# An eight-image ViT tower on one core: attention laid out anew, with values in 88-token chunks and even and odd heads in turn

## The chip, the cores and the metric

The kernel runs on one core of one Trainium2 chip. The metric is the device time in microseconds of one execution, lower is better. Times are medians over the runs shown.

## What is computed

Eight small images become 66 tokens each (two class tokens and 64 patches) of width 192. Tokens then pass one attention block with complex scores and a four-layer encoder. This is the reference, cut to the encoder layers that the change touches (B is 8, s is 66, H is 12 heads of DK = 64, F = 768, L = 4):

```python
for i in range(L):
    nx = t5_layer_norm(h, ln1[i])
    q = (nx @ attn_q[i]).reshape(b, s, H, DK)
    k = (nx @ attn_k[i]).reshape(b, s, H, DK)
    v = (nx @ attn_v[i]).reshape(b, s, H, DK)
    scores = jnp.einsum('bqhd,bkhd->bhqk', q, k) + bias
    attn = jax.nn.softmax(scores, axis=-1)
    ctx = jnp.einsum('bhqk,bkhd->bqhd', attn, v).reshape(b, s, H * DK)
    h = h + ctx @ attn_o[i]
    nx = t5_layer_norm(h, ln2[i])
    y = jax.nn.relu(nx @ ffn_wi[i]) @ ffn_wo[i]
    if i in MOE_LAYERS:        # layers 1 and 3, 8 experts, top 2
        y = y + moe_ffn(nx.reshape(-1, d), gate_w[mi], moe_w1[mi], moe_w2[mi]).reshape(b, s, d)
        mi += 1
    h = h + y
```

## The kernel before

Activations stay in SBUF, transposed: features on partitions, tokens on the free axis. The batch is cut into two halves of four images, NT = 264 tokens each; the first argument of nearly every stage is the half (0 or 1), and one half's small work is placed between the other half's large matmuls. The generator `stages()` yields one hand-written list of stages, and each engine walks that same list in the same order and issues its own part of each stage. So on every engine the order is that of the list; waits are semaphores with counts that are worked out from the list.

The stages that matter here, each for a half `hf` and a layer:

- `qk`: the queries (i = 0) or keys (i = 1), 6 groups of 5 matmuls with 264 columns. ACT copies each group from a bank of the family `pa` (three banks) to `qk`.
- `scores` for one image `b`: 12 products, one per head, with 64 rows of contraction (even heads on partitions 0 to 63, odd heads on 64 to 127), into the two banks `ps`. DVE adds the bias into `prob` (twice, L1227) and takes the maxima (L1062); POOL subtracts them (L622). With the next image's scores, ACT does the exponentials (L914), DVE the sums and reciprocals (L1067, L1068), POOL the scaling (L628). `scores_end` does these last three for image 3.
- `v` for one image: the values, tokens as stationary operand and 384 weight columns as moving one, 2 groups of 5 matmuls; ACT copies each group from `pa` to `vtok` (L1006).
- `tp`: 12 transposes of the probabilities into two `pa` banks, copied by ACT to `probT` (L909). `pv`: 12 products of `probT` and `vtok`, left by DVE in two parts in `wide` (L1238, L1239).
- `o_tail`, `o_main`: the output projection, 12 and 18 matmuls, added to `hT` by DVE.
- `squares` (ACT), `norm` (PE, then DVE L1084, then POOL L634) and `scale` (PE, then DVE L1102, L1072 to L1074) are the normalisation; the last of them makes `xs`, which the next `qk` or `hid` waits for.
- `hid` and `y_tail`, `y_main`: the feed-forward block; ACT writes each hidden group twice (L1022, L1023) and DVE subtracts (L1250). Its banks are shared with `pa` and `ps`.
- `split`: ACT (L934) and POOL (L613) cut loaded weights into two parts. `warm(n)`: n matmuls of 512 columns on zeros, whose result nobody reads.

In layers 0 and 2 all four `scores` and `v` of half 0 come before `qk` of half 1, and half 1's four scores are then interleaved with `tp` and `pv` of half 0. In layers 1 and 3 (with experts) the four `scores` and `v` of a half come in turn, then the six groups of `hid` of the other half (or of the same half), then `tp` and `pv`.

## Time and profile before

| | us |
|---|---|
| median of 3 runs | 766.58 (756.33 to 770.01) |
| the profiled execution | 758.47 |
| its span, first to last instruction | 755.7 |
| PE busy in it | 704.8 |
| DVE busy | 445.1 |
| ACT busy | 406.6 |
| POOL busy | 352.2 |
| mean granted TensorE clock | 0.972 of full |

PE is TensorE's matmuls, PEld its weight loads, DVE is VectorE, ACT ScalarE, POOL GpSimd. A span and a start are microseconds from the first instruction. Ends of matmuls are modelled, so the distance between the starts of two groups is a better price than the time beside a group. Instructions that issue a DMA are not counted as busy, though the engine spends time on them.

### The profile page before, as it was taken

The numbers are of one execution on the slowest core, as the hardware profiler recorded it, in microseconds if no ns is written. First come the engines' busy times: TensorE is split into PE (matmuls) and PEld (weight loads), VectorE is DVE, ScalarE is ACT, GpSimd is POOL, SyncE is SP. The second block draws the span as 40 slices with busy tenths as digits, with TensorE's granted clock in tenths as the row PEclk, the third lists the DMA queues.
The fourth block names the chain that finished last, engine by engine and source line by source line (L and its number), as shares of the span: only waits on it lengthen the run. The fifth ranks groups of instructions, "written<-read, shape, count | busy, mean of one in ns | idle before, by whom it ended". The sixth has DMA issues, their size and how long they took to land.

```text
span 755.7 us, 16388 instructions
## 1 busy us (share of the span) xinstructions
PE 704.8 (93%) x6735; PEld 626.9 (83%) x6735; DVE 445.1 (59%) x941; ACT 406.6 (54%) x913; POOL 352.2 (47%) x327
## 2 busy tenths in 40 slices
PE   6976999899899999899999999998999999999995
PEld 4853578788787989899999888887889898999995
DVE  0348435386556486676556645764765865666664
ACT  1387335542456365677767355444554647767642
POOL 2357525472466244336675333515743533544520
PEclk9997899998999999999999999989999999999998
DMA  7321001020220204243345030002211134233200
GB/s 211 88 74 43 2 2 33 1 85 1 69 78 18 59 3 131 81 126 116 119 143 147 3 84 1 2 2 74 74 43 33 28 105 123 83 116 91 89 1 22
DMA packets 36609, 49.20 MB, mean 65 GB/s; under 512 B 6155, under 2 KB 27575, under 8 KB 36023
## 3 DMA queue, kind: packets, MB, share of 16 engines
q1 hardware_dynamic: 33259, 43.49, 20.1%
q10 hardware_dynamic: 3276, 4.67, 2.0%
q8 instruction: 53, 0.87, 0.5%
q14 instruction: 21, 0.17, 0.1%
HBM read 47.70 MB, written 0.45 MB: 64 GB/s over the span
## 4 chain that ended last, share of the span: by engine, by line
PE 72%; DVE 9%; ACT 8%; POOL 5%; issue 3%; DMA 2%; SPq 0%; POOLq 0%; ACTq 0%; DVEq 0%
PE pd L684 35%; PE pa L684 23%; PE ps L684 9%; PE pa L715 4%; POOL w L613 1%; DVE xn L1102 1%; POOL prob L622 1%; ACT wide L1022 1%; POOL wo L613 1%; ACT w L934 1%; ACT wqkv L934 1%; DVE xs L1072 1%; DVE xs L1074 1%; ACT pa L1023 1%; ACT csq L983 1%
## 5 line engine op out<-in xcount | busy, mean ns | idle before, releaser
L613 POOL TENSOR_TENSOR w<-raw,w 128x384 fp32r<-128x384 f32 x140 | 141.8, 1015 | 132.0 <-ACT w L934 124.1
L684 PE MATMUL pd<-wide,w 128*128 128x264 f32 x1200 | 156.0, 286 | 0.1
L684 PEld LDWEIGHTS pd<-wide,w 128*128 128x128 f32 x1200 | 149.2, 188 | 0.9 <-DVE wide L1250 0.9
L684 PE MATMUL pa<-xs,w 128*128 128x264 f32 x810 | 120.7, 289 | 10.3 <-DVE wide L1250 6.6
L684 PEld LDWEIGHTS pa<-xs,w 128*128 128x128 f32 x810 | 107.1, 190 | 14.9 <-DVE wide L1250 8.6
L1250 DVE TENSOR_TENSOR wide<-pa,wide 128x264 fp32r<-128x264 f32 x144 | 62.1, 432 | 40.4 <-ACT pa L1023 38.0
L622 POOL TENSOR_TENSOR prob<-prob,mx 66x792 f32<-66x792 f32 x36 | 55.4, 1543 | 45.9 <-DVE mx L1062 45.6
L1022 ACT ACTIVATE wide<-pa 128x264 fp32r<-128x264 f32 x144 | 56.8, 394 | 35.0 <-PE pa L684 34.8
L628 POOL TENSOR_TENSOR prob<-prob,rc 66x792 f32<-66x792 f32 x36 | 54.4, 1513 | 44.1 <-DVE rc L1068 44.1
L684 PE MATMUL ps<-xs,w 128*128 128x264 f32 x480 | 74.3, 285 | 0.5 <-DVE prob L1227 0.5
L613 POOL TENSOR_TENSOR wqkv<-raw,wqkv 128x384 fp32r<-128x384 f32 x48 | 49.6, 1034 | 48.0 <-ACT wqkv L934 45.2
L1138 DVE TENSOR_TENSOR pd<-pd,vtok 128x264 f32<-128x264 f32 x64 | 43.6, 681 | 39.5 <-PE pd L684 39.4
L684 PE MATMUL pa<-xs,wqkv 128*128 128x264 f32 x480 | 61.7, 287 | 4.7 <-DVE xs L1074 4.0
L684 PEld LDWEIGHTS ps<-xs,w 128*128 128x128 f32 x480 | 64.6, 188 | 1.3 <-issue 1.2
L684 PEld LDWEIGHTS pa<-xs,wqkv 128*128 128x128 f32 x480 | 59.3, 188 | 7.6 <-DVE xs L1074 6.6
L684 PE MATMUL pa<-wqkv,xs 128*66 128x384 f32 x320 | 63.5, 345 | 0.0
L684 PE MATMUL pd<-warm_x,warm_w 128*128 128x512 bf16 x191 | 59.2, 429 | 0.0
L902 ACT ACTIVATE qk<-pa 128x264 f32<-128x264 f32 x102 | 39.4, 390 | 36.8 <-PE pa L684 36.5
L634 POOL TENSOR_TENSOR rs<-var,exponent 88x3 f32<-88x3 f32 x22 | 18.7, 849 | 85.6 <-DVE var L1084 85.6
L1023 ACT ACTIVATE pa<-pa 128x264 f32<-128x264 f32 x144 | 56.6, 393 | 0.0
L934 ACT ACTIVATE w<-raw 128x1536 fp32r<-128x1536 f32 (+1 forms) x40 | 52.6, 1321 | 7.4 <-PE pd L684 3.9
L1006 ACT ACTIVATE vtok<-pa 66x384 f32<-66x384 f32 x64 | 29.8, 482 | 46.5 <-PE pa L684 46.4
(126 smaller groups left out, 1149.4 us busy)
## 6 DMA issues: line engine op xcount, KB each, us to landing
raw<-in_moe_w_dram SPq DMA_DIRECT2D x16, 576.0 KB, 4.2
raw<-in_moe_w_dram SPq DMA_DIRECT2D x16, 384.0 KB, 3.5
raw<-in_moe_w_dram SPq DMA_DIRECT2D x32, 192.0 KB, 3.9
vtok<-cw_rows ACTq DMA_DIRECT2D x4, 1056.0 KB, 6.0
raw<-in_attn_o_dram SPq DMA_DIRECT2D x4, 576.0 KB, 4.0
raw<-in_ffn_wo_dram SPq DMA_DIRECT2D x4, 576.0 KB, 4.1
vtok<-in_patches_dram SPq DMA_DIRECT2D x2, 768.0 KB, 7.9
raw<-in_attn_q_dram SPq DMA_DIRECT2D x4, 384.0 KB, 3.6
```

Source lines behind the costliest of these rows:

```text
L613: ins = nc.gpsimd.tensor_tensor(low, whole, high.bitcast(F32), ALU.subtract)
L622: nc.gpsimd.tensor_tensor(p, p, m.unsqueeze(2).to_broadcast([S, H, S]), ALU.subtract).then_inc(sub_ready, 1)
L628: nc.gpsimd.tensor_tensor(p, p, r.unsqueeze(2).to_broadcast([S, H, S]), ALU.mult).then_inc(prob_ready, 1)
L684: return nc.tensor.matmul(out_ap, lhsT, rhs, start=first, stop=last)
L715: last = nc.tensor.transpose(bank[0:S, j * S:(j + 1) * S], probs(u)[:, g * HG + j, :], ident[0:S, 0:S])
L902: nc.scalar.activation(dst, src, ACT.Copy).then_inc(a_free, 1)
L934: nc.scalar.activation(hi, src, ACT.Copy).then_inc(chunk_hi, 1)
L1006: nc.scalar.activation(vtok[0:S, hf * HALF_B + b, n * F // 2:(n + 1) * F // 2], bank_a()[0:S, 0:F // 2], ACT.Copy).then_inc(a_free, 1)
L1022: nc.scalar.activation(wide[hf][:, 0, m, :], bank, gate_fn)
L1023: nc.scalar.activation(bank, bank, gate_fn).then_inc(h_ready, 1)
L1138: done(nc.vector.tensor_tensor(part, part, weight, ALU.mult))
L1250: nc.vector.tensor_tensor(wide[hf][:, 1, m, :], places["h"][n][0][:, 0:NT], wide[hf][:, 0, m, :].bitcast(F32), ALU.subtract).then_inc(h_fr ...
```

## The change

There are four parts; all are within the encoder layers.

1. `scores` takes both `ps` banks first and issues even and odd heads in turn, where before all six even heads came ahead of all six odd ones.
2. `v` is computed for three chunks of 88 tokens in place of four images of 66. ACT copies a chunk to a staging tile, waits for its own copy, and issues two DMAs that move the rows to their images in `vtok`. `pv` waits for these DMAs (`v_moved`). Staging reuses other tiles; for that half 1 gets queries and keys of its own (`qk_late`), and DVE waits for half 0's moves before its first `pv`.
3. The list is rearranged. In layers 0 and 2 half 1's `qk` moves between the scores, or behind the first `tp` and `pv`, of half 0; `o_tail` comes between half 1's scores; and image 3 of half 1 is transposed only after the feed-forward block of half 0. In layers 1 and 3 the two parts of `hid` come between scores, and `tp` of image 0 comes ahead of scores of image 3.
4. Of 191 `warm` matmuls 143 are left: 17 fewer in layer 0, 21 in layer 2, 5 in each of layers 1 and 3.

```diff
+VC, VCN = 3, NT // 3
+V_MOVES = (((0, 0, 0, S), (1, 0, S, VCN - S)),
+           ((1, VCN - S, 0, 2 * S - VCN), (2, 0, 2 * S - VCN, 2 * VCN - 2 * S)),
+           ((2, 2 * VCN - 2 * S, 0, 3 * S - 2 * VCN), (3, 0, 3 * S - 2 * VCN, S)))
+V_PARTS = (1, 2, 2, 1)
...
                 elif name == "v":
-                    b = stage[3]
+                    c = stage[3]
                     pe.wait_ge(chunk_split, chunks_until("qkv", stage[2], 2))
                     for n in range(2):
                         cols = slice(n * F // 2, (n + 1) * F // 2)
-                        tok = slice(b * S, (b + 1) * S)
+                        tok = slice(c * VCN, (c + 1) * VCN)
                         pairs = split_pairs(wqkv[:, 0, 2], wqkv[:, 1, 2], xs[hf][:, :, tok], cols)
-                        product(bank_a()[0:S, 0:F // 2], [(x, w) for w, x in pairs], a_full)
+                        product(bank_a()[0:VCN, 0:F // 2], [(x, w) for w, x in pairs], a_full)
...
                     cols = slice(b * S, (b + 1) * S)
-                    for g in range(2):
-                        bank = bank_s()
-                        row = slice(DK * g, DK * g + DK)
-                        for j in range(HG):
-                            last = mm(bank[0:S, j * S:(j + 1) * S], qk[row, 0, j, cols], qk[row, 1, j, cols], True, True)
-                        last.then_inc(s_full, 1)
+                    pair = [bank_s(), bank_s()]
+                    for j in range(HG):
+                        for g in range(2):
+                            row = slice(DK * g, DK * g + DK)
+                            last = mm(pair[g][0:S, j * S:(j + 1) * S], qk_of[hf][row, 0, j, cols], qk_of[hf][row, 1, j, cols], True, True)
+                            if j == HG - 1:
+                                last.then_inc(s_full, 1)
...
                     layer, b = stage[2:4]
-                    if b == 0:
-                        pe.wait_ge(a_free, groups_after(A_GROUPS, ("v", hf, layer, HALF_B - 1)))
+                    pe.wait_ge(v_moved[hf][b], 16 * V_PARTS[b] * (layer + 1))
...
                     for n in range(2):
-                        nc.scalar.activation(vtok[0:S, hf * HALF_B + b, n * F // 2:(n + 1) * F // 2], bank_a()[0:S, 0:F // 2],
+                        nc.scalar.activation(rows_of[:, c, n * F // 2:(n + 1) * F // 2], bank_a()[0:VCN, 0:F // 2],
                                              ACT.Copy).then_inc(a_free, 1)
+                    act.wait_ge(a_free, groups_after(A_GROUPS, stage))
+                    for b, to, at, rows in V_MOVES[c]:
+                        act.dma_start(vtok[to:to + rows, hf * HALF_B + b, :], rows_of[at:at + rows, c, :]).then_inc(v_moved[hf][b], 16)
...
                 elif name == "pv":
+                    if hf == 0 and stage[3] == 0 and stage[2]:
+                        for b in range(HALF_B):
+                            dve.wait_ge(v_moved[0][b], 16 * V_PARTS[b] * (stage[2] + 1))
```

The first place is PE at the head of layer 2, from the last of half 0's `qk` on. `ps<-qk` are scores, `pa<-wqkv,xs` values, `pa<-xs,wqkv` queries and keys, `pa<-ident,prob` transposes, `pd<-ident,rs` the `scale` matmuls. Before:

```order
L684 MATMUL ps<-qk 66x66 x12
L684 MATMUL pa<-wqkv,xs 66x384 x10
L684 MATMUL ps<-qk 66x66 x12
L684 MATMUL pd<-ident,rs 128x88 x3
L684 MATMUL pa<-wqkv,xs 66x384 x10
L684 MATMUL ps<-qk 66x66 x12
L684 MATMUL pa<-wqkv,xs 66x384 x10
L684 MATMUL ps<-qk 66x66 x12
L684 MATMUL pa<-wqkv,xs 66x384 x10
L684 MATMUL pd<-warm_x,warm_w 128x512 x6
L684 MATMUL pa<-xs,wqkv 128x264 x60
```

After the change the same stretch (from the second `scores` on) reads:

```order
L743 MATMUL ps<-qk 66x66 x12
L743 MATMUL pd<-ident,rs 128x88 x3
L743 MATMUL pa<-wqkv,xs 88x384 x10
L743 MATMUL ps<-qk 66x66 x12
L743 MATMUL pa<-xs,wqkv 128x264 x30
L774 MATMUL pa<-ident,prob 66x66 x12
L743 MATMUL ps<-qk 66x66 x12
L743 MATMUL pd<-probT,vtok 64x66 x12
L743 MATMUL pa<-xs,wqkv 128x264 x30
```

Half 1's queries have moved ahead of half 0's fourth scores, right behind the third, and no `warm` stands ahead of them.

The second place is ACT at the end of half 1's scores in layer 2: `sq<-hT` is `squares`, `probT<-pa` the copy behind `tp`, `prob<-prob` an exponential. After the change:

```order
L1066 ACTIVATE qk<-pa 88x384 [waits a_full] x2
L1070 DMA vtok<-qk 22x768 [waits a_free]
L1070 DMA vtok<-qk 66x768
L973 ACTIVATE prob<-prob 66x792 [waits sub_ready]
L1004 ACTIVATE sq<-hT 128x528 [waits d_full,d_free]
L968 ACTIVATE probT<-pa 66x396 [waits a_full] x4
```

Here `squares` stands ahead of the copies behind half 1's first two `tp`; in the list before it stood behind them. The two DMA rows are new on ACT's queue.

The third place is ACT in the first half of layer 3, between half 0's values and the end of the first part of `hid`, after the change (`wide<-ps`, `wide<-pa` are `hid`):

```order
L1066 ACTIVATE v_rows_wide<-pa 88x384 [waits a_full] x2
L1070 DMA vtok<-v_rows_wide 44x768 [waits a_free]
L1070 DMA vtok<-v_rows_wide 44x768
L973 ACTIVATE prob<-prob 66x792 [waits sub_ready]
L1088 ACTIVATE wide<-ps 128x264 [waits h_full]
L1089 ACTIVATE ps<-ps 128x264
L1088 ACTIVATE wide<-pa 128x264 [waits h_full]
L1089 ACTIVATE pa<-pa 128x264
```

The exponential of image 0 now stands behind two chunks' copies and four DMA issues, and `hid` behind it; before, `hid` came only after all values.

## Rows read from the trace of the kernel before

**Rows 1.** The page: the span, and PE's busy time and share.

```profile
span 755.7 us, 16388 instructions
PE 704.8 (93%) x6735; PEld 626.9 (83%) x6735; DVE 445.1 (59%) x941; ACT 406.6 (54%) x913; POOL 352.2 (47%) x327
```

**Rows 2.** Windows: length, busy PE, PEld, DVE, ACT, POOL, clock, DMA share, GB/s.

```profile
110.30:205.00 94.70, 88.12 (x907) 75.38 (x905) 52.88 (x100) 42.92 (x86) 45.34 (x38) 0.95 0.11 33
205.00:291.10 86.10, 84.34 (x919) 74.39 (x920) 54.26 (x120) 47.45 (x99) 45.95 (x39) 1.00 0.19 54
171.40:187.80 16.40, 16.37 (x191) 13.46 (x191) 10.11 (x21) 4.33 (x9) 3.18 (x3) 0.80 0.01 1
```

**Rows 3.** Groups by shape: xcount, busy us, mean ns of one, idle before and its releaser.

```profile
L684 PEld LDWEIGHTS pa<-xs,wqkv 128*128 128x128 f32 x480 | 59.3, 188 | 7.6 <-DVE xs L1074 6.6 <-ACT qk L902 0.7
...
L684 PEld LDWEIGHTS pa<-wqkv,xs 128*66 128x66 f32 x320 | 41.8, 138 | 11.8
...
L1006 ACT ACTIVATE vtok<-pa 66x384 f32<-66x384 f32 x64 | 29.8, 482 | 46.5 <-PE pa L684 46.4
```

**Rows 4.** The chain that ended last, layer 1: start, us, PE group of values.

```profile
265.29 1.89 PE pa L684 x10
```

**Rows 5.** PE timeline in layer 0: transposes, scores, pv, values, by starts.

```profile
154.75 0.86 PE L715 MATMUL pa<-ident,prob 66*66 66x66 f32 x12
155.53 1.47 PE L684 MATMUL ps<-qk 64*66 64x66 f32 x24
156.93 0.92 PE L684 MATMUL pd<-probT,vtok 66*64 66x66 f32 x24
157.78 1.95 PE L684 MATMUL pa<-wqkv,xs 128*66 128x384 f32 x10
```

**Rows 6.** The tile cw_rows: DMA issues on ACT's queue (ns min/median/max), landing (us).

```profile
L1030 ACTq DMA_DIRECT2D cw_rows<-cw x4: 312/320/576, 282.5 to 628.0; - x4
...
DMA to landing us min/median/max: 5.5/6.0/6.7
```

**Rows 7.** Timeline of layer 2: what half 1's queries wait for.

```profile
442.58 1.47 PE L684 MATMUL ps<-qk 64*66 64x66 f32 x24 [0.48 <-ACT qk L902]
...
447.41 1.28 ACT L914 ACT_TABLE_LOAD   x1
...
450.95 0.81 DVE L1102 SCALAR_TENSOR_TENSOR xn<-hT,vec,pd 128x264 f32<-128x264 f32 x2
...
453.72 0.43 DVE L1074 TENSOR_TENSOR xs<-xn,xs 64x264 fp32r<-64x264 f32 x1
...
458.01 1.47 PE L684 MATMUL pd<-warm_x,warm_w 128*128 128x512 bf16 x6
...
459.12 7.64 PE L684 MATMUL pa<-xs,wqkv 128*128 128x264 f32 x60
```

**Rows 8.** Timeline of layer 2: half 1's scores, hid, o_tail of half 1.

```profile
467.84 1.47 PE L684 MATMUL ps<-qk 64*66 64x66 f32 x24
...
505.44 0.96 PE L684 MATMUL pa<-xs,w 128*128 128x264 f32 x5
...
513.21 1.62 PE L684 MATMUL pd<-wide,wo 128*128 128x264 f32 x12
```

**Rows 9.** PE timeline: layer 3's first queries.

```profile
522.55 1.61 PE L684 MATMUL pa<-xs,wqkv 128*128 128x264 f32 x11 [1.53 <-DVE xs L1074]
```

**Rows 10.** The same columns as rows 2, for the second half of layer 1.

```profile
260.90:285.50 24.60, 24.60 (x263) 21.65 (x263) 22.48 (x57) 13.82 (x30) 12.51 (x10) 1.00 0.03 6
```

**Rows 11.** DVE timeline, layer 1: y_main's add of half 1, then of half 0.

```profile
239.36 0.43 DVE L1142 TENSOR_TENSOR hT<-pd,hT 128x264 f32<-128x264 f32 x1
...
247.38 0.43 DVE L1074 TENSOR_TENSOR xs<-xn,xs 64x264 fp32r<-64x264 f32 x1
...
285.05 0.43 DVE L1142 TENSOR_TENSOR hT<-pd,hT 128x264 f32<-128x264 f32 x1
```

**Rows 12.** The same columns, instructions that touch the tile prob alone.

```profile
260.00:276.00 16.00, 0.00 (x0) 0.00 (x0) 10.59 (x15) 2.60 (x3) 9.48 (x7) 1.00 0.01 4
```

More of the change, by code:

```diff
@@ L174, in stages @@
                 yield ("squares", 1, "encoder")
-                beside = [[("norm", "encoder", 0)], [("scale", "encoder", 0), ("squares", "ln1")], [("norm", "ln1", 0)], [("scale", "ln1", 0)]]
-            else:
-                beside = [[("norm", "ln1", layer)], [("scale", "ln1", layer)], [], []]
-            for b in range(HALF_B):
-                yield ("scores", 0, layer, b)
-                for x in beside[b]:
-                    yield (x[0], 1) + x[1:]
-                yield ("v", 0, layer, b)
@@ new lines, in stages @@
+                yield ("v", 0, 0, 0)
+                yield ("norm", 1, "encoder", 0)
+                yield ("v", 0, 0, 1)
+                yield ("scores", 0, 0, 1)
+                yield ("scale", 1, "encoder", 0)
+                yield ("squares", 1, "ln1")
+                yield ("v", 0, 0, 2)
+                yield ("scores", 0, 0, 2)
+                yield ("norm", 1, "ln1", 0)
+                yield ("tp", 0, 0, 0)
+                yield from warm(2)
+                yield ("pv", 0, 0, 0)
@@ L195, in stages @@
+            yield ("squares", 0, "ln2")
             yield ("tp", 1, layer, 0)
-            yield ("o_tail", 0, layer)
+            yield from warm(2)
             yield ("pv", 1, layer, 0)
+            yield ("norm", 0, "ln2", layer)
             yield ("tp", 1, layer, 1)
             yield ("scores_end", 1, layer)
-            yield ("o_main", 0, layer)
-            yield ("squares", 0, "ln2")
-            yield from warm(1)
+            yield from warm(2)
             yield ("pv", 1, layer, 1)
@@ L204, in stages @@
             yield ("tp", 1, layer, 2)
[L205 removed]
+            yield ("scale", 0, "ln2", layer)
             yield ("pv", 1, layer, 2)
[L207 to L211 removed]
+            yield from warm(2)
             yield from hid(0, layer, 0)
@@ L215, in stages @@
             yield ("squares", 0, "ln1")
+            yield ("tp", 1, layer, 3)
+            yield from warm(2)
+            yield ("pv", 1, layer, 3)
             yield ("o_tail", 1, layer)
```

133 lines of the change are left out of this document (89 added, 44 removed).

## The prediction, made before the changed kernel was run

> **What bounds the kernel now.** I read the page's totals first. PE is busy for 704.8 us of a span of 755.7 us, 93%, and no other engine passes 59% [rows 1]. That says where to look, not what a saved matmul is worth, so I read windows over single stages next. Layer 0, from its first queries to those of layer 1, is 94.7 us long with PE busy for 88.1; layer 1's attention and first feed-forward part is 86.1 us long with PE busy for 84.3 [rows 2]. There is nearly no idle time on PE in either. But a shorter window tells more: in the second half of layer 1, from the first bias add to the end of the first feed-forward block, DVE is busy for 22.5 of 24.6 us [rows 10]. There PE and DVE finish together, and work that leaves PE alone buys little. (The windows' order of engines is PE, PEld, DVE, ACT, POOL.)
>
> Last I read the timeline around the waits. In layer 2 half 1's `xs` are ready at 453.72 + 0.43 = 454.15, yet PE takes its queries only at 459.12, since all of half 0's scores and values stand ahead [rows 7]. That is what the rearrangement uses. At layer 2's end it is the other way about: `hid` at 505.44, `o_tail` of half 1 at 513.21 and layer 3's queries at 522.55, the last behind a wait of 1.53 us for DVE's `xs` [rows 8, 9]. One more thing stands in the windows: the stretch 171.4 to 187.8 of layer 0, all transposes, `pv` and `warm`, ran at a granted clock of 0.80, so part of it at 1.2 GHz where the layer else has 2.4 [rows 2].
>
> **The terms on PE.** Scores of one image take 156.93 - 155.53 = 1.40 us before, and transposes 0.78 (155.53 - 154.75) [rows 5]. No row of before shows twelve heads alternating between the two halves of the rows. The nearest is `pv`: also twelve f32 products of 66 columns, whose outputs alternate between partitions 0 to 63 and 64 to 127; it takes 157.78 - 156.93 = 0.85 us [rows 5]. The ends are 1.40 (no overlap at all) and 0.70 (two heads always at once). I take 0.85, a gain of 0.55 on each of 8 x 4 = 32 images, 17.6 us.
>
> A rule of the Trainium skill bears on this: TensorEngine Tiling (Array Packing), Theoretical Speedup, gives up to 2x for a small dimension of at most 64. By that rule the term would be 32 x 0.70 = 22.4 us; by the `pv` row it is 17.6. I keep the row's.
>
> Values: ten matmuls, one stage, take 1.89 us [rows 4]. A layer had eight such stages and now has six; 8 fewer in all, 15.1 us. Against this the stationary part has 88 columns, not 66. Weight loads take 138 ns with 66 and 188 with 128 [rows 3], so 88 cost about 18 ns more; if nothing hid that, 240 matmuls would give back 4.3 us. Loads lie beside matmuls mostly, so I take nothing, and keep 10.8 to 15.1.
>
> `warm`: six take 459.12 - 458.01 = 1.11 us [rows 7], so 48 fewer are 8.9 us of PE. Where they only filled a wait this is worth nothing; I count it only inside the stages below.
>
> Together 17.6 + 15.1 + 8.9 = 41.6 us of PE. If PE alone set the time, 758.5 would become 716.9.
>
> **What is added.** ACT's copies fall from 64 to 48, each 0.48 us [rows 3], 7.7 us less. It gets 48 DMA issues. ACT's issues take 0.32 us in the median and 0.58 at most [rows 6]: 15.4 to 27.6 us, at a guess 0.4 each, so 0.8 us per chunk, plus a wait of some 0.1 for its own copy. ACT is a queue in order: behind these stand the exponential, then `hid`. The landing I bound by the 6.7 us of the slowest DMA of that queue [rows 6]; `pv` of an image comes 8 us and more after its chunk, so landing costs nothing. Without that cover it would be up to 6 us in each of 8 half-layers.
>
> **Layer 2, step by step.** Scores of image 0 start at 442.6 [rows 7]. PE then has three scores (2.6 us), three chunks of values (5.7), and the small matmuls of `norm` and `scale` (about 1.6): it is out of work at 452.5. On ACT, two chunks' copies and four DMA issues end at about 449.6; only then comes the table load of 1.28, which stood at 447.41 before [rows 7], and the exponential (0.9): 451.8. DVE's sum and reciprocal take 1.2; then the scaling takes 454.15 - 450.95 = 3.2 us as before [rows 7]: `xs` at 456.2. PE waits some 3.6 us there. Then come 7.3 us of queries and keys, two transposes (1.6), one scores (0.85), two `pv` (1.7) and a bare wait of 0.7 for the copy of the second transposes: half 1's scores start at 468.3, not at 467.84 [rows 8], with two `tp` and two `pv` already done.
>
> From there to `hid` it was 505.44 - 467.84 = 37.6 us [rows 8]. It loses 2.2 (scores), 3.8 (values), 1.9 (ten `warm`), 4.1 (a transpose of half 0, two of its `pv`, and image 3 of half 1, moved out), and about 2.5 of slow clock as in the alike stretch of layer 0: 23.1. New waits come in: `squares` stands ahead of the copies of half 1's first transposes on ACT and waits for DVE to add `o_main`, behind a bias add, a maximum and a sum (2.5 us); `xs` come late, behind the last sum and the two passes over a `pv` on DVE (3 us). So 28.7, and `hid` at 497.0. Then 7.8 us to the end of the block, as before [rows 8], and the moved image in the open: transposes, two `warm`, copy, `pv` and DVE's two passes, 3.7 us. `o_tail` at 508.5 for 513.21, and unchanged 9.3 us after it [rows 8, 9] layer 3 at 517.8: **4.7 us gained**.
>
> **Layer 0.** Same list, but half 1's `xs` need four dependent small stages. They now queue behind chunk copies on ACT and behind a scaling of probabilities on POOL, so I put them at 141.0, about 2 us later than before. With both `tp` and `pv` done ahead, scores of half 1 come at 148.4, and with layer 2's 49.5 us from there layer 1 starts at 197.9 in place of 205.0 [rows 2]: **7 us gained**.
>
> **Layers 1 and 3.** First half: DVE needs about 3 us of softmax per image (15 of 16 long instructions of four images are 10.59 us [rows 12], and a short one each besides). With that four times, the scaling, six `hid` subtractions, the tail's add and one `pv` it has from 214 on some 22 us in a row, so `y_main` of half 1 can be added at 236.2 at best where it was at 239.36 [rows 11]; with ACT's queue (third piece of the order) I put it at 237.8. But behind it `tp` of image 1 waits for `squares`, and POOL makes the root only behind a scaling, so `xs`, 247.81 before [rows 11], come at 247.3: 0.5 gained. Second half: DVE keeps its 22.5 busy of 24.6 us [rows 10], so at most about 2 up to 285.05 [rows 11] and something behind it, where the three `pv` no longer wait: 2.5. Two layers, **6 us gained**.
>
> **The clock.** The new waits of 2 to 4 us are of a kind that this trace has few of, and after thin stretches it shows a clock of 0.80 over 16.4 us, 3.3 us lost [rows 2]. I charge 2 us in each of layers 0 and 2: **4 us lost**.
>
> **The sum.** 758.5 - 4.7 - 7.0 - 6.0 + 4.0 = 744.8 us against the profiled execution's own 758.47. Its median neighbours are higher (756.33 to 770.01, median 766.58), so the ratio of 0.982 gives 752.8 us. About 28 of 41.6 us taken off PE turn into waits.
>
> **The rivals.**
> - *PE decides all the same.* For it speak 97% busy PE in layer 1 [rows 2] and that DVE's 22.5 us contain short gaps. Then most of 41.6 us comes through: 22 to 41 us, say 30, so 736. The clock loss would be gone as well.
> - *Evacuation decides.* The Trainium skill, TensorEngine Tiling, PSUM Bottleneck, says that tiling speeds up TensorE but not the evacuation of PSUM. By the windows, as a mechanism of this kernel: DVE's softmax per image is 3 us [rows 12] where PE's scores and values per image fall from 3.3 to 2.3, so DVE sets the pace of all 32 images; with the 15 us of ACT's issues on that path too, gain 0 to 6, 762. The trace agrees with the rule in layer 1's second half [rows 10].
> - *No overlap.* Scores stay at 1.40: only the values are left, and if half of their 15.1 us hides, the gain is 7.5: 759.
> - *Slower.* The place is the rearranged stretch of layers 0 and 2. PE waits for half 1's `xs` and again for `squares`; if the granted clock falls to 1.2 GHz in each such wait and stays there for the queries behind it, 7.3 us of them take 14.6. Twice per layer in two layers this is up to 29 us, and with it the gains above are gone from about 14 us on; at 29 it ends at 774. For it: 0.80 in a stretch with no long wait at all [rows 2]. Against it: large matmuls bring the clock back.
>
> **How the numbers follow.** A gain of 6 to 22 us, the forecast, has a chance of 0.46; PE decides 0.22; evacuation or no overlap 0.14; slower 0.18. A measurement of this kernel can tell about 2% from no change, 15.3 us here, which cuts my forecast case in two: 0.21 above it, 0.25 below. Faster by over 2%: 0.21 + 0.22 = 0.43. Slower by over 2%: 0.15 of the 0.18. The rest, 0.42, is within 2%. For the range I take PE decides at 33 us (733) and the slower case at its middle (771), which leaves out about 2 in 10. The forecast's own range is 744 to 761.
>
> **What would show it.** In the changed profile: scores groups of 12 at starts 0.8 to 0.9 us apart from what follows; values 1.9 us per ten, 240 matmuls; PE waiting 3 to 4 us for L1074's counterpart ahead of half 1's queries in layer 2; a wait of 2 to 3 us for `probT` behind half 1's first transposes; ACT's DMA issues near 0.4 us, none of their landings waited for; PE's busy share falling below 93%. It is wrong if the scores take over 1.1 us, if PE stays back to back in layers 1 and 3, or if whole stretches of queries run at half clock.

## The result, and the profile of the changed kernel

The changed kernel takes **803.0 us** (median of 4 runs, 799.6 to 805.0), the kernel before 765.95 us beside it: a ratio of **1.052** (95% interval 1.042 to 1.063). It is slower by 5%, and lies above the range given (733 to 771). The medians of the kernel before differ a little from one set of runs to the next (760.5 to 766.0), so kernels of different sets are compared by their ratios below; one per cent is 7.6 us. Medians are over all runs of a kernel, ratios over its fast runs alone.

The page of the changed kernel: its span, the busy time of each engine, the granted clock in 40 slices, the DMA queue of ACT, and the chain of waits.

```profile
span 802.6 us, 16186 instructions
PE 720.4 (90%) x6607; PEld 647.1 (81%) x6607; DVE 442.1 (55%) x941; ACT 400.3 (50%) x897; POOL 351.6 (44%) x327
...
PEclk9977898797798896999999998976979889999998
...
q10 hardware_dynamic: 5916, 11.16, 4.6%
...
PE 60%; DVE 14%; ACT 11%; POOL 5%; issue 4%; ACTq 3%; DMA 2%; SPq 0%; POOLq 0%; DVEq 0%
```

PE has less to do and is busy longer, 720.4 us against 704.8 [rows 1]. That is the mark of a clock at half speed, and the slices show it, with 7 and 8 where the kernel before had 9. Windows say where. The first window is layer 0, the second layer 1's attention and first feed-forward part, the fourth layer 2 (columns as in [rows 2]):

```profile
113.50:214.40 100.90, 90.75 (x872) 79.59 (x872) 53.29 (x101) 41.09 (x82) 45.34 (x38) 0.80 0.16 47
214.40:314.30 99.90, 86.32 (x890) 76.59 (x890) 52.43 (x119) 46.04 (x95) 47.27 (x40) 0.87 0.23 70
314.30:463.00 148.70, 140.42 (x1119) 137.47 (x1117) 93.00 (x211) 92.33 (x231) 73.35 (x73) 0.99 0.34 101
463.00:552.80 89.80, 80.07 (x831) 71.58 (x832) 50.79 (x94) 36.91 (x77) 35.07 (x28) 0.84 0.14 40
```

Layer 0 went from 94.7 us at a clock of 0.95 to 100.9 at 0.80, and layer 1's stretch, which was at 1.00 [rows 2], to 0.87. The experts' part of layer 1, whose code did not change, stands at 0.99. What PE waits for, from the table of waits (total, times, longest):

```profile
PE pa L743 <- DVE wide L1319: 13.1, 9, 3.2
PE pd L743 <- ACT probT L968: 10.0, 8, 2.2
PE pa L743 <- DVE xs L1140: 6.8, 5, 4.1
...
PE pa L774 <- POOL prob L687: 5.4, 3, 2.7
```

PE's timeline at three places, layer 0's first scores and values, layer 1's first half, and layer 2 from half 1's first queries on (start, duration, count, and the wait before it):

```profile
121.88 0.94 PE L743 MATMUL ps<-qk 64*66 64x66 f32 x24
122.75 1.97 PE L743 MATMUL pa<-wqkv,xs 128*88 128x384 f32 x10
...
228.29 0.94 PE L743 MATMUL ps<-qk 64*66 64x66 f32 x24
230.04 0.85 PE L743 MATMUL ps<-xs,w 128*128 128x264 f32 x5 [0.81 <-DVE prob L1293]
...
235.34 2.24 PE L743 MATMUL pa<-wqkv,xs 128*88 128x384 f32 x10 [3.23 <-DVE wide L1319]
237.50 1.62 PE L743 MATMUL ps<-qk 64*66 64x66 f32 x24
...
243.19 0.85 PE L774 MATMUL pa<-ident,prob 66*66 66x66 f32 x12 [1.54 <-DVE wide L1319]
...
483.33 6.62 PE L743 MATMUL pa<-xs,wqkv 128*128 128x264 f32 x30 [4.10 <-DVE xs L1140]
492.29 3.91 PE L743 MATMUL pa<-xs,wqkv 128*128 128x264 f32 x30
...
518.14 0.92 PE L743 MATMUL pd<-probT,vtok 66*64 66x66 f32 x24 [2.16 <-ACT probT L968]
```

The same scores take 0.94 us ahead of the wait of 3.23 us and 1.62 behind it. The thirty matmuls of queries take 6.62 us behind their wait of 4.10; the thirty of the keys, which have the same shape, take 3.91 behind them. ACT at the second of these places:

```profile
230.83 1.56 ACTq L1070 DMA_DIRECT2D vtok<-v_rows_wide  x2
232.44 0.86 ACT L973 ACTIVATE prob<-prob 66x792 f32<-66x792 f32 x1 [1.64 <-issue]
233.21 0.37 ACT L1088 ACTIVATE wide<-ps 128x264 fp32r<-128x264 f32 x1
```

Two moves are issued in 1.56 us, and the exponential and the copies of `hid` stand behind them; DVE's subtraction needs those copies, and PE's values the bank that it frees. In e4 below, where ACT issues no move, PE's wait at this place is 1.19 us in place of 3.23. All 48 issues, by their line (minimum, median and maximum in ns), and the exponential's waits for them:

```profile
L1070 ACTq DMA_DIRECT2D vtok<-qk x24: 757/770/791, 162.9 to 625.8; - x24
L1070 ACTq DMA_DIRECT2D vtok<-v_rows_wide x18: 757/770/948, 227.2 to 577.1; - x18
L1070 ACTq DMA_DIRECT2D vtok<-v_rows_first x6: 757/786/1391, 125.3 to 135.0; - x6
...
ACT prob L973 <- issue: 18.8, 11, 2.1
```

### The profile page after: what moved, and what is told of

It is laid out like the page before. It is cut to its first block, busy times and chain, and to the rows that moved or that the text cites. A ratio compares the mean times of both kernels' runs of the same rounds, so it can differ in the third digit from the quotient of the medians.

```text
span 802.6 us, 16186 instructions
## 1 busy us (share of the span) xinstructions
PE 720.4 (90%) x6607; PEld 647.1 (81%) x6607; DVE 442.1 (55%) x941; ACT 400.3 (50%) x897; POOL 351.6 (44%) x327
## 4 chain that ended last, share of the span: by engine, by line
PE 60%; DVE 14%; ACT 11%; POOL 5%; issue 4%; ACTq 3%; DMA 2%; SPq 0%; POOLq 0%; DVEq 0%
PE pd L743 30%; PE pa L743 19%; PE ps L743 7%; ACTq L1070 3%; PE pa L774 3%; POOL w L672 2%; DVE rc L1133 2%; DVE prob L1293 2%; DVE mx L1128 2%; ACT prob L973 1%; ACT wide L1088 1%; DVE hT L1218 1%; POOL wqkv L672 1%; ACT w L993 1%; ACT wqkv L993 1%
## 5 line engine op out<-in xcount | busy, mean ns | idle before, releaser
L743 PE MATMUL pa<-xs,w 128*128 128x264 f32 x810 | 128.1, 300 | 11.2 <-DVE wide L1319 7.6
L743 PEld LDWEIGHTS pa<-xs,w 128*128 128x128 f32 x810 | 113.5, 201 | 17.0 <-DVE wide L1319 9.6
L681 POOL TENSOR_TENSOR prob<-prob,mx 66x792 f32<-66x792 f32 x36 | 55.3, 1540 | 91.8 <-DVE mx L1128 91.8
L743 PE MATMUL pa<-xs,wqkv 128*128 128x264 f32 x480 | 70.1, 309 | 8.7 <-DVE xs L1140 6.8
L743 PE MATMUL ps<-xs,w 128*128 128x264 f32 x480 | 76.4, 290 | 1.6 <-DVE prob L1293 1.6
L743 PEld LDWEIGHTS pa<-xs,wqkv 128*128 128x128 f32 x480 | 67.3, 212 | 11.1 <-DVE xs L1140 8.6
L743 PEld LDWEIGHTS ps<-xs,w 128*128 128x128 f32 x480 | 66.6, 194 | 2.2 <-issue 1.8
L1004 ACT ACTIVATE sq<-hT 128x528 f32<-128x528 f32 x18 | 11.6, 646 | 92.9 <-DVE hT L1208 88.5
L1293 DVE TENSOR_TENSOR prob<-ps,bias 66x396 f32<-66x396 f32 x64 | 33.3, 560 | 44.8 <-PE ps L743 44.5
L743 PE MATMUL pd<-warm_x,warm_w 128*128 128x512 bf16 x143 | 54.1, 495 | 0.0
L743 PE MATMUL pa<-wqkv,xs 128*88 128x384 f32 x240 | 48.1, 346 | 6.5 <-DVE wide L1319 5.5
```

The source lines that it names most:

```text
L681: nc.gpsimd.tensor_tensor(p, p, m.unsqueeze(2).to_broadcast([S, H, S]), ALU.subtract).then_inc(sub_ready, 1)
L743: return nc.tensor.matmul(out_ap, lhsT, rhs, start=first, stop=last)
L1293: nc.vector.tensor_tensor(prob[:, b, heads, :], bank_s()[0:S, 0:HG * S].rearrange("p (h n) -> p h n", h=HG), bias[:, heads, ::-1], ALU.add ...
```

## The experiments

**Theory:** the loss is made of three things: ACT's time for the issues, PE's clock behind new waits, and the rearranged list itself. **Rivals:** the chunks or the new scores cost the time by themselves; the clock explains all of it; or layers 0 and 2, where the prediction put its risk, hold the loss.

| run | median us | ratio to before | 95% interval | clock |
|---|---|---|---|---|
| changed kernel | 803.0 | 1.052 | 1.042 to 1.063 | 0.896 |
| e1 scores only | 758.2 | 0.997 | 0.992 to 1.002 | 0.980 |
| e15 changed, scores not in turn | 803.6 | 1.056 | 1.047 to 1.064 | 0.902 |
| e3 old list, chunks, ACT moves | 774.7 | 1.018 | 1.008 to 1.028 | 0.950 |
| e9 old list, chunks, SP moves | 761.4 | 1.002 | 0.997 to 1.006 | 0.948 |
| e4 changed, SP moves | 786.7 | 1.032 | 1.023 to 1.041 | 0.904 |
| e6 changed list, no chunks | 791.9 | 1.042 | 1.035 to 1.049 | 0.923 |
| e7a list in layers 0, 2 only | 767.0 | 1.010 | 1.006 to 1.013 | 0.952 |
| e7b list in layers 1, 3 only | 777.9 | 1.017 | 1.008 to 1.026 | 0.943 |
| e10 changed, waits filled | 777.4 | 1.022 | 1.015 to 1.030 | 0.954 |
| e11 e10 with SP moves | 767.0 | 1.009 | 1.005 to 1.013 | 0.971 |
| e12 e9 with waits filled | 767.9 | 1.008 | 1.004 to 1.012 | 0.952 |
| e16 e7b with waits filled | 779.5 | 1.022 | 1.017 to 1.027 | 0.949 |
| e17 e1, hid between scores | 756.2 | 0.993 | 0.989 to 0.997 | 0.979 |
| e18 e1, image 3 late | 779.2 | 1.025 | 1.016 to 1.033 | 0.948 |
| e21 changed, image 3 undone | 791.2 | 1.039 | 1.033 to 1.045 | 0.910 |
| **e19** best | **751.6** | **0.987** | 0.983 to 0.991 | 0.963 |
| e22 e19 without its fill | 765.0 | 1.006 | 1.003 to 1.009 | 0.934 |
| e20 e19 with e17's order | 771.4 | 1.013 | 1.008 to 1.017 | 0.951 |

The clock is that of the profiled execution, which is not always near the median: e1's took 748.9 us, e19's 758.6, e12's 773.9 and e16's 790.5, the last with a clock of 0.79 ahead of layer 0. So stretches inside layers are read from the profiles below, and not whole times.

### The scores

**e1** is the kernel before with scores in turn alone; **e15** is the changed kernel with the old order inside an image:

```diff
-                    for g in range(2):
-                        bank = bank_s()
-                        row = slice(DK * g, DK * g + DK)
-                        for j in range(HG):
...
+                    pair = [bank_s(), bank_s()]
+                    for j in range(HG):
+                        for g in range(2):
+                            row = slice(DK * g, DK * g + DK)
...
```

> The kernel before with one edit: scores of even and odd heads in turn; list, values and warm as before. In the changed kernel twelve heads took 0.87 us (121.88 to 122.75) where they took 1.40, so PE has 17 us less to do. Theory ISSUE (the changed kernel is slower for the DMA issues on ACT, 0.77 us each, 48 of them): none are here, so a gain, 5 to 15 us, 751 to 761, wherever DVE's softmax does not set the pace. Theory CLOCK (waits that the shorter PE work opens let the granted clock fall): the time is the same or slower, 766 to 780, and the mean clock falls well below 0.972. Theory ORDER (the rearranged list opens the waits): as ISSUE.

> The changed kernel with the heads' scores in the old order inside each image (all even heads, then all odd), everything else as changed. PE's scores go back from 0.87 to 1.40 us, 17 us more of PE. Theory A (waits and clock decide, not PE): most of these 17 us fall into waits, 803 to 806 us, and a clock slightly higher since PE is busier. Theory B (PE's time counts in the new order as it did in the old): 815 us or more. Under 800 would say that the faster scores themselves cost time through the clock.

e15's scores of an image take 1.39 us again (122.65 - 121.26), the changed kernel's 0.87:

```profile
121.26 1.47 PE L743 MATMUL ps<-qk 64*66 64x66 f32 x24
122.65 1.98 PE L743 MATMUL pa<-wqkv,xs 128*88 128x384 f32 x10
```

Some 17 us of PE are worth 0.3% in the old list, where 1.000 lies inside the interval, and nothing that can be told in the new one. PE's saving isn't the loss, and over the whole kernel it isn't a gain that these runs can tell. In e1 PE waits more for a bank of the scores, which DVE's first pass over an image frees (1.2 us in three waits before):

```profile
PE ps L684 <- DVE prob L1228: 4.1, 9, 1.3
```

The stages differ, though. From first queries to the next layer's, layers 0 and 2 take 91.05 and 83.9 us in e1, at clocks of 0.98 and 1.00, where they took 94.7 and 88.8 at 0.95 and 0.96; layer 0 takes 91.0 in e17 and e18 too. Layer 1's attention takes 86.9 where it took 87.4. So what gain there is lies in layers 0 and 2, in part through the clock, and layers 1 and 3 have none.

### The chunks and the queue of their moves

**e3** has the changed kernel's body with the list and the `warm` of before. **e4** is the changed kernel and **e9** is e3, both with the moves issued on SP's queue, in the order of the list between SP's loads:

```diff
-                    act.wait_ge(a_free, groups_after(A_GROUPS, stage))
-                    for b, to, at, rows in V_MOVES[c]:
-                        act.dma_start(vtok[...], rows_of[at:at + rows, c, :]).then_inc(v_moved[hf][b], 16)
...
+                elif stage[0] == "v":
+                    hf, layer, c = stage[1:4]
+                    sp.wait_ge(a_free, groups_after(A_GROUPS, stage))
+                    for b, to, at, rows in V_MOVES[c]:
+                        sp.dma_start(vtok[...], v_rows(hf, layer)[at:at + rows, c, :]).then_inc(v_moved[hf][b], 16)
```

> The changed kernel with the list of the kernel before (values in three chunks at the places of images 0 to 2; warm as before): scores in turn, chunks and DMA moves are in, only the rearrangement and the fewer warm are out. ORDER expects it faster than before, 740 to 755, since PE lost 32 us of work and no new wait came. ISSUE expects most of the loss still there: 37 us more on ACT less 7.7 us of copies, part of it hidden, 780 to 800. CLOCK expects between, 765 to 785, with a clock of 0.90 to 0.94.

> e3 (scores in turn, chunks and moves, with the old list and old warm; 774.7) with the 48 moves on SP's queue. If the 16 us between e1 (758) and e3 are ACT's DMA issues, this is 748 to 760, since values in chunks save PE 15 us. If they are waits of pv for the moves, or contention with the weight loads, 770 to 780.

> The changed kernel with one edit: the 48 moves are issued on SP's queue, between the weight loads in the list's order, and ACT issues none. ISSUE expects 765 to 780: 37 us leave ACT, most of them on the way of the exponentials and of the feed-forward copies. ORDER and CLOCK expect 795 to 803, as the waits for half 1's xs and for the copies behind squares stay.

Chunks with moves on ACT cost 2.1% (e3 against e1). On SP they cost 0.5% (e9), within what the intervals leave open. In the new list SP's queue takes back 2.0% (e4 against the changed kernel), less than was expected of the issues (765 to 780 us). So ACT's issues cost some 12 us in the old list (e3 against e9) and 15 in the new one, each with more than 1% of doubt, and eight stages fewer of values, 15 us of PE, bring nothing. In e4 PE's wait behind the first part of `hid` in layer 1 has shrunk from 3.23 us to

```profile
229.97 1.95 PE L758 MATMUL pa<-wqkv,xs 128*88 128x384 f32 x10 [1.19 <-DVE wide L1331]
```

The Trainium skill, DMA: Bandwidth & Descriptors, Issuing engines are not separate DMA queues, says that issuing DMAs on several engines saves only the time on the sequencer that it takes to initiate them, and calls this usually small beside the DMA itself. e4 agrees with the first part. The profile has no landing times of these moves, so the second can't be held against it; but 0.77 us each is not small where ACT works in order in front of a softmax.

### The list, by layers

**e6** is the changed kernel with values per image and no moves. **e7a** is e6 with the old list in layers 1 and 3, **e7b** with the old list in layers 0 and 2.

```diff
         yield ("v", 0, layer, 2)
+        yield ("v", 0, layer, 3)
         yield ("scores", 0, layer, 2)
```

> The changed kernel's list, scores in turn and warm, but values per image of 66 tokens straight to their place, image 3 right behind image 2: no staging, no moves. PE has 15 us more to do than the changed kernel. ISSUE expects 765 to 785, near the run with the moves on SP. ORDER expects 790 to 805: the rearranged list alone is enough. CLOCK expects the time to go with the mean clock: at 0.90 it is 795, at 0.95 775.

> The run e6 (scores in turn, values per image, no moves) with the list of the kernel before for layers 1 and 3, so that only layers 0 and 2 are rearranged (with 38 warm fewer). e1, which has the old list in all layers, took 758, and e6 792. If the loss of the rearrangement sits where PE waits for half 1's xs in layers 0 and 2, as my prediction had it, this is 780 to 790. If it sits in layers 1 and 3, 762 to 772.

> The same the other way about: only layers 1 and 3 are rearranged (10 warm fewer), layers 0 and 2 keep the old list. If feed-forward between scores puts ACT's and DVE's work for hid ahead of the softmax and is the loss, 778 to 788; if the loss is in layers 0 and 2, 760 to 768. This and e7a together should give e1 plus 34 us if the two parts do not touch each other.

The list costs 4.5% (e6 against e1), 34 us, with no chunk and no move in it: 1.3% alone in layers 0 and 2, 2.0% alone in layers 1 and 3. The rest of 1.2% shows only with both, and is no more than the four intervals together leave open. In all of these "the list" takes in the 48 `warm` matmuls that went with it (38 in layers 0 and 2, 10 in layers 1 and 3): no run has the new order with the old `warm`, so the two are not separated. The prediction had gains at both places, and no loss at all in layers 1 and 3.

### The clock, or the waits themselves

**e10** is the changed kernel with 156 more `warm` matmuls, put ahead of the stages for which PE waits; **e11** is e10 with moves on SP; **e16** is e7b with 92 of them; **e12** is e9 with 6 to 16 at each long wait.

```diff
+        yield from warm(14)
         yield ("v", 0, layer, 2)
         yield ("scores", 0, layer, 2)
...
+                yield from warm(18)
                 yield ("qk", 1, layer, 0)
```

> The changed kernel with 156 more warm matmuls (0.2 us each, on zeros) at the places where its PE waited over 0.8 us in layers 0 to 3, about as many as fill each wait. Nothing waits less for it. CLOCK (half clock behind the waits is most of the loss) expects a mean clock of 0.95 or more and 770 to 785. If the waits themselves are the loss, the clock may rise but the time stays at 795 to 810, as the fillers take PE's time for nothing.

> The changed kernel with both repairs at once: the 48 moves issued on SP's queue (alone 803.0 became 786.7) and 156 more warm matmuls in PE's waits (alone 777.4). Theory A, the two losses are separate things, ACT's issue time on the chain and the clock behind PE's waits: the gains add, 777.4 - 16 = 761 us, granted clock 0.95 or more. Theory B, both repairs mend the same thing (with SP's issue the waits get shorter, and the fill then has little to fill or even delays PE): 771 to 778 us. If a third loss sits in the order itself, the time stays over 758 even at a clock of 0.95, and layer 1's stretch from its second queries to the last output products stays longer than the 87 us of before.

> Only layers 1 and 3 rearranged, values per image, no moves (777.9 us, clock 0.943; 20 us over the same kernel with the old list), and 92 more warm matmuls in the waits of these layers' attention. If the rearrangement there costs through the clock alone: about 760 us at a clock of 0.97 or more. If the waits themselves cost (hid products behind more of the softmax on DVE, later images' transposes behind POOL): 768 to 773 us, with layer 1's stretch still some 6 us longer than the 87 of before though its matmuls run at full speed.

> The old list with chunks of values, moves on SP's queue, scores in turn (761.4 us, clock 0.948), and 8 to 16 more warm matmuls at each of its long waits of PE (2.0 and 2.3 us for xs in layer 0, 2.8 before the output products of layers 0 and 2, 3.2 before the hid products of layers 1 and 3). If the clock is what keeps it from gaining: 5 to 10 us less, 751 to 756, clock 0.97 or more, and faster than before. If DVE's softmax sets the pace, the waits are as long as before and only the matmuls right behind them get faster: 758 to 762.

More work on PE takes 3.0% off the time (e10 against the changed kernel) and lifts the clock from 0.896 to 0.954: some 23 us hung on the clock. In the profiles most of it is in layers 1 and 3, whose stretches (as below) go from 103.4 and 102.4 us to 94.2 and 95.6. With SP's queue as well it is 4.3%; the two repairs give 5.0% when added, so they overlap by little. The Trainium skill, TensorE: Matmul & The Clock Gate, A second HAM failure mode: psum-queue depth-cycling, says that short pauses between groups of matmuls can make the clock go back and forth. The rows at 235.34 and 237.50 agree.

But the clock is not all. The stretch of layer 1 from its first queries to half 1's last output products, of before, e1, e16, e11 and the changed kernel in turn:

```profile
204.98:292.34 87.36, 85.61 (x929) 75.65 (x930) 55.16 (x122) 48.46 (x103) 47.11 (x40) 1.00 0.20 59
```

```profile
200.97:287.85 86.88, 82.04 (x930) 71.49 (x930) 55.02 (x122) 48.11 (x103) 47.34 (x40) 1.00 0.20 60
```

```profile
215.38:311.69 96.31, 92.02 (x970) 77.04 (x971) 53.70 (x122) 48.95 (x103) 47.31 (x40) 0.98 0.19 56
```

```profile
201.24:294.32 93.08, 87.41 (x951) 74.30 (x952) 53.68 (x122) 47.12 (x99) 47.29 (x40) 1.00 0.26 75
```

```profile
214.36:317.75 103.39, 89.81 (x905) 80.08 (x905) 54.19 (x123) 47.39 (x99) 47.27 (x40) 0.86 0.24 73
```

At a clock of 1.00 the new order still takes 93.1 us, 6 us more than before. How much of the 6 is the order and how much the 46 filling matmuls in the stretch (951 where the changed kernel has 905) is not separated. e16 says the same without chunks: the fill lifts the clock of this stretch from 0.89 (e7b) to 0.98 and shortens it only from 97.6 to 96.3, and no gain shows in the median, which lies above both expectations. e12 missed both of its expectations as well: it is 0.7% above e9, and why is not shown. Its profile has layers 0 and 2 longer, 105.0 and 94.6 us at 0.90 and 0.89 where e9 has 100.0 and 85.2 at 0.90 and 0.96, and layer 1's stretch shorter, 85.4 for 87.9; but that execution was 6 us above e12's median, so the place of the loss is likely and not certain. The fill is no gain everywhere.

### Which stage of layers 1 and 3

**e17** and **e18** each take one part of the rearrangement into e1's kernel (half 1 alike; values per image). e17:

```diff
-        for b in range(HALF_B):
-            yield ("scores", 0, layer, b)
-            yield ("v", 0, layer, b)
...
-        yield from hid(1, layer - 1, 0)
...
+        yield ("scores", 0, layer, 1)
+        yield ("v", 0, layer, 1)
+        yield ("hid", 1, layer - 1, 0, 0)
+        yield ("scores", 0, layer, 2)
+        yield ("v", 0, layer, 2)
+        yield ("hid", 1, layer - 1, 0, 1)
+        yield ("scores", 0, layer, 3)
+        yield ("v", 0, layer, 3)
```

e18:

```diff
-        for b in range(HALF_B):
+        for b in range(HALF_B - 1):
...
         yield from hid(1, layer - 1, 0)
+        yield ("v", 0, layer, 3)
         yield ("tp", 0, layer, 0)
-        yield ("scores_end", 0, layer)
+        yield ("scores", 0, layer, 3)
         yield ("y_tail", 1, layer - 1, 0)
         yield ("pv", 0, layer, 0)
-        yield ("tp", 0, layer, 1)
         yield ("split", None, "w1", layer, 0)
         yield ("y_main", 1, layer - 1, 0)
         yield ("squares", 1, "ln1")
+        yield ("tp", 0, layer, 1)
+        yield ("scores_end", 0, layer)
```

> The kernel of e1 (before with scores in turn, 758.2 us; layer 1 takes 42.9 us from its first queries to half 1's, then 7.4, then 36 to half 1's last output products) with one thing of the rearranged list in layers 1 and 3: the two hid groups stand between scores 1 and 2 and between 2 and 3, not behind all scores. Theory H (the hid groups tie a bank of the scores and DVE's and ACT's order to the softmax): most of the 20 us that the rearrangement of these layers costs is here, 768 to 778 us. Theory S (the fourth image's scores behind the first transposes cost it): 756 to 761.

> The kernel of e1 with the other thing in layers 1 and 3: the scores of image 3 behind the transposes of image 0, and the second transposes and the last sum behind the main y products. Theory S (image 3's softmax starts 3 to 5 us later, and its transposes at the end of each half wait for POOL's share of it): 768 to 778 us. Theory H: 756 to 761. If neither costs alone, the two together do.

e18 costs 2.8% against e1, e17 nothing (its stretch of layer 1 is 88.7 us for e1's 86.9). The timeline of e18 (ACT and PE) in layer 1, whose queries began at 205.88:

```profile
239.33 0.64 ACT L950 ACTIVATE sq<-hT 128x528 f32<-128x528 f32 x1 [4.65 <-DVE hT L1147]
239.88 0.86 ACT L914 ACTIVATE probT<-pa 66x396 f32<-66x396 f32 x2
240.50 0.92 PE L688 MATMUL pd<-probT,vtok 66*64 66x66 f32 x24 [1.68 <-ACT probT L914]
240.64 0.86 ACT L919 ACTIVATE prob<-prob 66x792 f32<-66x792 f32 x1
...
296.01 0.88 PE L719 MATMUL pa<-ident,prob 66*66 66x66 f32 x12 [2.28 <-POOL prob L632]
```

and e1's ACT, whose queries began at 200.97:

```profile
230.39 0.86 ACT L915 ACTIVATE prob<-prob 66x792 f32<-66x792 f32 x1
...
235.85 0.65 ACT L946 ACTIVATE sq<-hT 128x528 f32<-128x528 f32 x1 [0.81 <-DVE hT L1143]
```

In e1 image 3's exponential comes 29.4 us after the first queries, ahead of the squares. In e18 it comes after 34.8 us, queued behind squares that waited 4.65 us for DVE, and behind the copy of the second transposes. Its sum and POOL's scaling follow later still, and PE waits 1.68 us for `probT` there, and 2.28 for POOL in half 1. The stretch takes 95.9 us where e1's takes 86.9, and its clock is 0.93 for 1.00, so part of the 9 us is again the clock. The changed kernel shows the same order on ACT, in layer 1, whose queries began at 214.36:

```profile
251.43 0.64 ACT L1004 ACTIVATE sq<-hT 128x528 f32<-128x528 f32 x1 [4.68 <-DVE hT L1208]
251.98 0.87 ACT L968 ACTIVATE probT<-pa 66x396 f32<-66x396 f32 x2
252.74 0.86 ACT L973 ACTIVATE prob<-prob 66x792 f32<-66x792 f32 x1
```

Half 0's last exponential comes 38.4 us after the first queries; in the kernel before it was 29.4, as in e1. e18 moves the scores of image 3, its values behind `hid`, and also the second transposes with the last sum; which of them weighs most is not separated.

**e21** undoes this in the changed kernel, ACT's moves and all else kept:

```diff
+        yield ("scores", 0, layer, 3)
         yield ("tp", 0, layer, 0)
-        yield ("scores", 0, layer, 3)
+        yield ("scores_end", 0, layer)
         yield ("y_tail", 1, layer - 1, 0)
         yield ("pv", 0, layer, 0)
+        yield ("tp", 0, layer, 1)
         yield ("split", None, "w1", layer, 0)
         yield ("y_main", 1, layer - 1, 0)
         yield ("squares", 1, "ln1")
-        yield ("tp", 0, layer, 1)
-        yield ("scores_end", 0, layer)
```

> The changed kernel (803.0 us) with one thing undone in layers 1 and 3: the scores of image 3 stand again ahead of the transposes of image 0 and (in half 0) the second transposes and the last sum again ahead of the main y products and the squares. Moves stay on ACT, the other queries' order stays. If what e18 showed on the old kernel (21 us) is the same loss here: 779 to 786 us, with layer 1 some 8 us shorter than the 103 of the changed kernel. If in the changed kernel the late moves on ACT's queue hold this stretch anyway: 795 us or more.

It takes back 1.3%, 10 us, half of what e18 cost and less than the 779 to 786 us expected; with the two intervals it may be anything from next to nothing to 2.5%. The stage says it more firmly: layer 1's stretch is 97.2 us, 6.2 shorter than in the changed kernel, but 10 longer than before. Now PE waits, in half 0, for the scores' own bank:

```profile
246.39 0.94 PE L743 MATMUL ps<-qk 64*66 64x66 f32 x24 [2.50 <-DVE wide L1319]
```

This is the other half of the rearrangement: `hid` between scores. It was free in e17, where a stage of values stands between each of these stages and the next, behind image 3's scores too. With three chunks there is none behind image 3's scores. That this cover is what makes the difference is read from the two lists, and not tested by itself.

### The version that beats both

**e19** has the rearranged list in layers 0 and 2 and the old one in layers 1 and 3, with chunks, scores in turn, moves on SP's queue and e10's and e12's fill. **e22** is e19 without the added `warm` (108 matmuls, not the 67 of its expectation). **e20** is e19 with e17's order in layers 1 and 3:

```diff
         for b in range(HALF_B):
+            if b > 1:
+                yield from warm(7)
             yield ("scores", 0, layer, b)
             if b < VC:
                 yield ("v", 0, layer, b)
+            if b in (1, 2):
+                yield ("hid", 1, layer - 1, 0, b - 1)
-        yield from warm(16)
-        yield from hid(1, layer - 1, 0)
```

> The changed kernel with both repairs (e11, 767.0 us) and the old list in layers 1 and 3, chunks of values kept, with 22 warm matmuls per such layer in its waits as in e12. In e11 layer 1 took 93.1 us from its first queries to the last output products, in e12 85.4. If the rest of the loss is that order: 2 x 7.7 less, 751 to 753 us, faster than before by 1%. If it is not, 762 to 767.

> e19 (751.6 us) without any of its 67 added warm matmuls: chunks, moves on SP's queue, scores in turn, rearranged list in layers 0 and 2 alone. If the fill is worth in layers 0 and 2 what it was in the changed kernel as a whole (25.6 us for four layers, 19.7 with SP's queue): 760 to 768 us at a clock near 0.93. If the waits that let the clock fall were mostly those of layers 1 and 3, whose order is undone here: 752 to 757.

> e19 (751.6 us) with the hid groups between the scores in layers 1 and 3, as in e17, where this took 2.1 us off; fill put at the places where PE then waits. The parts add: 748 to 751 us, ratio to before 0.982 to 0.987. If the longer stretch of scores without hid groups no longer binds: 751 to 753.

e19 came out at 751.6 us, 1.3% faster than before, as was expected from e11's and e12's stretches of layer 1. The same stretch in e19, e22 and e20:

```profile
213.29:298.66 85.37, 82.17 (x925) 72.14 (x932) 54.51 (x122) 46.64 (x99) 47.08 (x40) 1.00 0.27 79
```

```profile
209.33:296.11 86.78, 79.91 (x909) 71.51 (x910) 54.69 (x122) 46.88 (x99) 47.06 (x40) 0.98 0.26 77
```

```profile
204.81:301.61 96.80, 91.16 (x934) 78.72 (x934) 56.11 (x122) 47.13 (x99) 47.39 (x40) 0.91 0.24 72
```

The fill is worth 1.9% (e22 against e19), and layer 0 shows it best: 91.5 us at a clock of 0.98 in e19, 96.5 at 0.84 in e22. In layer 1 it is 1.4 us. e20 missed its expectation by 18 us and more: e17's order, with its fill moved, costs 11.4 us in this stretch once values come in three chunks, at a clock of 0.91.

Is the rearranged list of layers 0 and 2 a gain by itself? Layer 0 in e9, e12, e22 and e19 in turn:

```profile
115.41:215.45 100.04, 85.32 (x886) 73.91 (x885) 52.60 (x100) 41.14 (x82) 45.24 (x38) 0.90 0.15 47
```

```profile
113.92:218.94 105.02, 95.17 (x934) 78.66 (x933) 52.17 (x100) 41.15 (x82) 45.21 (x38) 0.90 0.15 45
```

```profile
112.88:209.33 96.45, 85.78 (x872) 75.90 (x872) 53.10 (x101) 41.21 (x82) 45.25 (x38) 0.84 0.17 49
```

```profile
121.83:213.29 91.46, 80.71 (x895) 69.21 (x902) 53.19 (x101) 40.94 (x82) 45.33 (x38) 0.98 0.19 51
```

Against e1, which has the old list and values per image and takes 91.05 us here, nothing is gained. Without fill the new list is no gain with chunks either: e22 is 0.4% above e9, with a shorter layer 0 (96.5 for 100.0) and a longer layer 2 (91.8 for 85.2). With fill it is: e12 and e19 differ in the list of layers 0 and 2 and the places of the fill there, and e19 is 2.1% faster. The profiles, of which e12's is a long one, have 91.5 us for 105.0 in layer 0 and 84.2 for 94.6 in layer 2. Whether the order does it or the better placed fill is not separated.

## Why the prediction was wrong, point by point

**Right: PE's terms.** Scores take 0.87 us (122.75 - 121.88) for 0.85 predicted. The 240 matmuls of values take 48.1 us of PE where 320 took 63.5, and no price of the 88 columns shows in them; their weight loads take 155 ns for the 138 of before, as estimated, and hide. The rival "PE decides all the same" is ruled out by e15, where the same 17 us given back to PE change nothing. (The 97% that it names for PE in layer 1 are 98% by [rows 2].)

**Wrong size: ACT's issues.** The step "at a guess 0.4 each" came from the transfer of another tile on the same queue, `cw_rows<-cw` [rows 6]. The real ones take 0.77 us, 37 us in all, above even the upper bound of 27.6. e4 and e9 show that this costs 12 to 15 us; the forecast had it covered.

**Wrong: layers 1 and 3, "6 us gained".** This is the step that failed. The prediction saw that `tp` of image 1 would wait for the squares, and carried this to half 1's `xs`, but not to what stands behind the squares on ACT: image 3's exponential, on which the last transposes of the half rest. It counted DVE's busy time (22 us in a row) where the order of ACT and POOL set the end. Layer 1's stretch went from 87.4 to 103.4 us and layer 3's from 87.1 to 102.4: 31 us lost of the 46 by which the two profiled executions differ. Neither half gained: in layer 1 the first, up to half 1's queries, took 50.2 us for 42.9, the second 53.2 for 44.5. e18 shows 21 us for image 3's place (with what it moves along) in both layers on the old kernel, and e21 shows about 10 of them in the changed one. The rest of the 31 us is ACT's issues, the clock behind the waits, and `hid` between scores once values come in chunks; these overlap, and no run splits them cleanly.

**Wrong size: the clock, "4 us lost".** It was charged to layers 0 and 2 alone. e10 shows 23 us, and layer 1, which had stood at 1.00, fell to 0.86. The rival "slower" had the mechanism and its place in layers 0 and 2 right (waits for `xs` and `squares`, half speed behind them: 6.62 us for thirty matmuls of queries). Its chance of 0.18 and its end of 774 us were too low, since it left out layers 1 and 3 and ACT's issues. The end was also reckoned from the profiled execution's 758.5 us and not, as the other rivals and the range, from the median of 766.6; on that it is 782, and still too low.

**Right in kind: layer 2's waits.** PE was to wait 3.6 us for half 1's `xs` and waits 4.10; 2.5 us behind the squares were predicted, 2.16 measured (at 518.14, for `probT`). But the sum went wrong by the clock. From layer 2's first queries to layer 3's it was 88.8 us and is 92.2, where 84.1 was forecast. Layer 0 was to gain 7 us and lost 6.2.

**The rival "evacuation decides" (762 us)** is what happened where the list was left alone and the moves were on SP: e1 and e9 lie within 0.5% of before, with up to 32 us less on PE (17.6 and 15.1 of the forecast's terms, the first measured as 17). The Trainium skill, TensorEngine Tiling (Array Packing), PSUM Bottleneck, says that tiling speeds up TensorE but not the evacuation of PSUM. e1's longer waits for `prob` agree with it in kind, but make up only 3 of the 17 us; and the clock had a part as well, 0.948 in e9's profile where it was 0.972.

## What to carry to other kernels

Where several engines work in a fixed order, follow each moved stage into every queue and ask what now stands behind it: the largest loss that a single tested part of the rearrangement showed here was an exponential behind a waiting square, and no engine's sum of busy time shows it. Work saved on PE is worth little when a softmax on three other engines paces it, and the pauses that replace it can halve the clock of what follows; where they must be, fill them. Issue small moves from a queue that nothing waits for, and measure one issue of that very transfer before the change.

## What the runs showed of the hardware

- Issuing a move from one on-chip tile to another costs 0.77 us of ACT's time in the median, where the issues of `cw_rows<-cw` on the same queue cost 0.32 [rows 6]. Size doesn't set it: the 24 moves out of `qk`, eight each of 66, 132 and 198 KB, all lie between 0.757 and 0.791. The longest of all 48 took 1.39.
- In the changed kernel layer 0 stands at a granted clock of 0.80 though none of PE's waits in it is longer than 2.2 us, and layers 1 and 2, with waits of up to 3.2 and 4.1 us, at 0.86 and 0.84. Added throwaway matmuls in such waits bring the whole kernel from 0.896 to 0.954, with less time in spite of more work (e10); in e12 they did not.
- The part ahead of layer 0 is the same in all kernels but for 4 `warm` matmuls, and yet layer 0's first queries begin anywhere from 109.9 us (e1) to 121.8 (e19) and 124.3 (e16) in the profiled executions. The granted clock of this part goes with it: 0.88 in the changed kernel (113.5 us), 0.80 in e19, 0.79 in e16. Stretches inside a layer repeat far better (85.37 and 85.40 us for layer 1 in e19 and e12; 91.0 to 91.1 for layer 0 in e1, e17, e18 and e16, though e7b with the same layer 0 has 93.8).
